# Values projected for four pairs of heads at once and kept in DRAM, and the rope's sine product taken before the halves are swapped

## The reference

```
hn = (h - mean) * rsqrt(var + 1e-5) * gamma + beta
q, k, v = hn @ Wq + bq, hn @ Wk + bk, hn @ Wv + bv        # 16 heads of 64
q, k = rope(q), rope(k)       # x * cos + concat(-x[32:], x[:32]) * sin, in each head
attn = softmax(causal(q @ k.T / 8))
x = layernorm(h + (attn @ v) @ Wo + bo + h)
gate, up = x @ (w_gate / 127).T, x @ (w_up / 127).T
x = layernorm(x + (silu(gate) * up) @ (w_down / 127).T + x)
```

## Time and profile before

| | |
|---|---|
| median of three runs | 2310.25 us (2309.42 to 2313.67) |
| profiled execution, its own time | 2305.9 us |
| its span in the profile | 2304.1 us |
| PE busy | 2144.3 us, 93% of the span |
| DVE busy | 1691.7 us, 73% |
| POOL busy | 1435.4 us, 62% |
| ACT busy | 958.2 us, 42% |
| granted TensorE clock, mean | 0.973 |

### The profile page before, as it was taken

One profiled execution on the slowest core, in us unless ns is written; L12 is line 12 of the kernel. 1 busy time (PEld: TensorE's weight loads), 2 busy tenths in 40 slices (PEclk: granted clock), 3 DMA queues, 4 the chain that ended last, 5 costly groups with the idle time before them and its releaser, 6 DMA issues.

```text
span 2304.1 us, 43543 instructions
## 1 busy us (share of the span) xinstructions
PE 2144.3 (93%) x15872; PEld 1407.3 (61%) x15872; DVE 1691.7 (73%) x2318; ACT 958.2 (42%) x1301; POOL 1435.4 (62%) x1204
## 2 busy tenths in 40 slices
PE   5779999999999999899999999999999999889997
PEld 4446565556565656455656565556565654789996
DVE  8567878787878787777877777787777775466654
ACT  3334444444434443434444444444344445333433
POOL 2447777777777777566868686878687779200000
PEclk8799999999999999989999999999999999899999
DMA  5100101010101011101111111111111130222200
GB/s 161 63 22 19 46 19 46 21 43 22 42 24 41 24 41 54 48 19 32 33 32 33 32 33 33 33 32 33 33 29 36 29 115 10 96 92 73 100 19 28
DMA packets 79484, 100.45 MB, mean 44 GB/s; under 512 B 13984, under 2 KB 43680, under 8 KB 79008
## 3 DMA queue, kind: packets, MB, share of 16 engines
q1 hardware_dynamic: 79264, 97.60, 14.2%
HBM read 40.93 MB, written 23.07 MB: 28 GB/s over the span
## 4 chain that ended last, share of the span: by engine, by line
PE 73%; DVE 17%; issue 6%; ACT 1%; DMA 1%; SPq 1%; POOL 1%; DVEq 0%; ACTq 0%
PE o_ps L1150 17%; PE m_ps L1098 8%; DVE mpart L748 6%; PE x_ps L1053 6%; PE s_ps L1119 4%; PE x_ps L1055 4%; PE x_ps L1054 4%; PE s_ps L1121 4%; PE s_ps L1125 4%; PE s_ps L1123 4%; PE gu_ps L1053 2%; PE gu_ps L1054 2%; PE gu_ps L1055 2%; PE x_ps L1157 1%; DVE rot L787 1%
## 5 line engine op out<-in xcount | busy, mean ns | idle before, releaser
L474 POOL TENSOR_TENSOR acc<-acc,pt 128x512 f32<-128x512 f32 (+3 forms) x1024 | 1235.4, 1238 | 232.6 <-ACT pt L533 232.0
L748 DVE TENSOR_REDUCE mpart<-m_ps 128x2 f32<-128x1024 f32 (+2 forms) x576 | 625.6, 1086 | 342.1 <-PE m_ps L1098 205.5
L533 ACT ACTIVATE pt<-s_ps 128x1024 f32<-128x1024 f32 (+3 forms) x640 | 545.1, 896 | 561.7 <-PE s_ps L1125 319.5
L1150 PE MATMUL o_ps<-pt,v 128*64 128x512 f32 (+3 forms) x2560 | 555.4, 556 | 0.0
L1098 PE MATMUL m_ps<-qk 64*128 64x512 f32 (+3 forms) x1280 | 285.8, 442 | 102.5 <-DVE mpart L748 85.1
L1098 PEld LDWEIGHTS m_ps<-qk 64*128 64x128 f32 x1280 | 121.8, 186 | 384.0 <-issue 217.3
L1150 PEld LDWEIGHTS o_ps<-pt,v 128*64 128x64 f32 x2560 | 158.5, 139 | 232.5 <-issue 211.4
L469 POOL TENSOR_TENSOR acc<-pt 128x512 f32<-128x512 f32 (+1 forms) x128 | 165.5, 1313 | 200.0 <-ACT pt L533 200.0
L1119 PE MATMUL s_ps<-qk 64*128 64x512 f32 (+3 forms) x1280 | 249.8, 385 | 0.0
L1121 PE MATMUL s_ps<-qk 64*128 64x512 f32 (+3 forms) x1280 | 235.9, 363 | 0.0
L1125 PE MATMUL s_ps<-aux,ones_r 64*128 64x512 f32 (+3 forms) x1280 | 235.8, 362 | 0.0
(11 more groups left out here) (161 smaller groups left out, 3406.7 us busy)
## 6 DMA issues: line engine op xcount, KB each, us to landing
rot<-qr SPq DMA_DIRECT2D x512, 64.0 KB, 2.0
attn<-o_n SPq DMA_DIRECT2D x64, 256.0 KB, 2.1
o_raw<-attn SPq DMA_DIRECT2D x8, 2048.0 KB, 9.0
w_raw<-in_wqkv SPq DMA_DIRECT2D x51, 128.0 KB, 2.6
h_g<-in_h SPq DMA_DIRECT2D x8, 512.0 KB, 3.6
out<-out_g SPq DMA_DIRECT2D x7, 512.0 KB, 2.9
qk_place<-in_h SPq DMA_DIRECT2D x4, 512.0 KB, 5.8
pt<-in_h SPq DMA_DIRECT2D x4, 512.0 KB, 10.6
```

The costliest lines, as they stand in the source:

```text
L474: nc.gpsimd.tensor_tensor(sums, sums, probs, ALU.add).then_inc(summed, 1)
L533: nc.scalar.activation(pt[:, u % SLOTS, :, q0:NB], s_ps[:, two:two + 2, q0:NB], ACT.Exp, scale=SCALE)\
L748: nc.vector.tensor_reduce(dst, m_ps[:, :, 0:w], AX.X, ALU.max, negate=True).then_inc(maxed, 1)
L1150: last = nc.tensor.matmul(o_ps[rows, q0:NB], v[par][:, j, rows], pt[:, u % SLOTS, a, q0:NB], start=(j == 0), stop=(j == n - 1), skip_group ...
```

## The change

It has four parts that go together.

1. **Values.** They are projected for four pairs of heads at once: one tile of 128 rows against 512 columns of `Wv` (six matmuls of 512 columns, `project_v`), 16 tiles for each set of four pairs, four sets in all. ACT brings a tile out of PSUM without its bias (`evict_v`) into one buffer, `v_part`, and SP stores it in DRAM, `v_far` (256 KB a tile). Each pair loads its own 128 columns of it, 12 tiles at group 1 of the pair before and 4 tiles at its own group 2 (`load_v`). The first set is projected ahead of pair 0, four tiles after each block; the second in pairs 0 to 3, one tile in each of the old places of values; the third, which needs the second batch row, in pair 7 alone (`SWITCH_PLACES`, 16 places); the fourth in pairs 8 to 11. Pairs 4 to 6 and 12 to 15 project no values. `Wv` has its own buffers and is split in two halves at a time (`WV_LOAD`, `WV_SPLIT`).
2. **Rope.** `products` on DVE takes both products straight out of PSUM, first the one with the sine into `qr` (its signs are now those of the half from which it comes), then the one with the cosine. The swap then carries a finished product, and in place of two instructions after the maxima there is one, the sum (`turned_sum`). ACT has no `piece_raw` any more.
3. **Bias of values.** The probabilities of a row sum to 1, so the bias is added to the result of attention, where it is split for the output projection (`attn_hi`, `attn_lo`).
4. **Unfolding.** `each_pair` has no hardware loops any more. The buffers `r_b` and `o_n` are gone: the division is made in place in `o_sum`, and ACT waits for the store of `o_sum` before it writes it again.

```diff
-VALUES = {g: int(x[1]) for g, x in XUSE.items() if x[0] == "V"}
+V_GROUPS = [g for g, x in XUSE.items() if x[0] == "V"]
+SWITCH_PLACES = [(3, 1), (4, 1), (5, 1), (7, 1), (8, 1), (9, 0), (9, 1), (10, 1), (11, 1), (13, 1), (14, 0), (14, 1),
+                 (15, 1), (16, 0), (16, 1), (17, 1)]
+V_PIECES = {it: {} for it in range(2 * PAIRS)}
+for it in range(4):
+    V_PIECES[it] = {(g, 0): (TT + 4 * it + i, 4 * it + i) for i, g in enumerate(V_GROUPS)}
+    V_PIECES[PAIRS + it] = {(g, 0): (3 * TT + 4 * it + i, 4 * it + i) for i, g in enumerate(V_GROUPS)}
+V_PIECES[PAIRS - 1] = {place: (2 * TT + i, i) for i, place in enumerate(SWITCH_PLACES)}
+WV_LOAD = {(0, 2): 2, (0, 5): 3, (5, 3): 4, (5, 6): 5, (8, 2): 6, (8, 5): 7}
+WV_SPLIT = {(0, 4): 2, (0, 7): 3, (5, 5): 4, (5, 8): 5, (8, 4): 6, (8, 7): 7}
...
-            pair(FIRST, 0, 0, 0, 0)
-            with engine.Fori(0, PAIRS // 2 - 1) as two:
-                pair(MIDDLE, two * 2 + 1, 1, two * 2 + 1, 0)
-                pair(MIDDLE, two * 2 + 2, 0, two * 2 + 2, 0)
...
+            kinds = {0: FIRST, PAIRS - 1: SWITCH, 2 * PAIRS - 1: LAST}
+            for it in range(2 * PAIRS):
+                pair(kinds.get(it, MIDDLE), it, it % 2, it % PAIRS, it // PAIRS)
...
+            def load_v(it, c0, c1, done):
+
+                here, cols = slice(TG * c0, TG * c1), slice(it % 4 * P, (it % 4 + 1) * P)
+                sp.dma_start(v[it % 2][:, here, :], v_far[it // 4, here, :, cols].rearrange("t p n -> p t n"))\
+                  .then_inc(done, 16)
+
+            def store_v(it, place):
+                if place in V_PIECES[it]:
+                    n, t = V_PIECES[it][place]
+                    sp.wait_ge(v_done, n + 1)
+                    sp.dma_start(v_far[n // TT, t, :, :], v_part[:, :]).then_inc(v_stored, 16)
...
                     if g in PIECE and kind is not LAST:
                         swap_halves(it + 1, *PIECE[g])
+                    store_v(it, (g, 0))
+                    store_v(it, (g, 1))
+                    if kind is SWITCH and g == 14:
+                        sp.wait_ge(v_stored, 16 * v_stored_for(it + 1, 2))
+                        load_v(it + 1, 0, 3, v_in)
...
-            def piece_raw(n, c, a, par, i, first=False):
...
-                act.wait_ge(qk_proj, n * (2 * BLOCKS) + (2 * c + a + 1))
-                nc.scalar.activation(qr[:, a, :], qk_bank[i][a], ACT.Identity, bias=b_qk[:, par, a:a + 1])\
-                  .then_inc(qk_raw, 1)
...
             def evict_o(n, blk):
                 act.wait_ge(pv_done, n * NG + (BLOCK_ENDS[blk] + 1))
-                act.wait_ge(normed, n * BLOCKS + (blk + 1))
+                act.wait_ge(o_stored, (n * BLOCKS + blk) * 16 + 16)
...
+            def evict_v(n, bank, dst):
+                act.wait_ge(v_proj, n + 1)
+                nc.scalar.activation(dst, bank, ACT.Copy).then_inc(v_done, 1)
...
+            def evict_v_piece(it, place):
+                if place in V_PIECES[it]:
+                    n = V_PIECES[it][place][0]
+                    if n > TT:
+                        act.wait_ge(v_stored, 16 * (n - TT))
+                    evict_v(n, x_ps[:, :], v_part[:, :])
...
-                nc.vector.tensor_tensor(v[par][:, TG * c:TG * (c + 1), :],
-                                        v_bank[i].rearrange("p (t n) -> p t n", t=TG),
-                                        b_v[:, par, :].unsqueeze(1).broadcast_to([P, TG, P]), ALU.add)\
-                  .then_inc(v_done, 1)
-
-            def cosine(n, c, a, par, i):
...
+            def products(n, c, a, par, i):
+
+                if c == 0 and a == 0:
+                    dve.wait_ge(b_in, n * 16 + 16)
+                dve.wait_ge(qk_proj, n * (2 * BLOCKS) + (2 * c + a + 1))
+                nc.vector.scalar_tensor_tensor(qr[:, a, :], qk_bank[i][a], b_qk[:, par, a:a + 1],
+                                               sin_sb[:, NB * c:NB * (c + 1)], ALU.add, ALU.mult).then_inc(qk_raw, 1)
...
-                nc.vector.tensor_tensor(rot[:, a, :], rot[:, a, :], sin_sb[:, NB * c:NB * (c + 1)], ALU.mult)\
-                  .then_inc(rope_mul, 1)
...
-            def project_v(n, c, i):
-                for t in range(TG):
-                    here = slice(NB * c + P * t, NB * c + P * (t + 1))
-                    for k in range(KC):
-                        last = product(v_bank[i][:, t * P:(t + 1) * P], [hn[:, x, k, here] for x in range(2)],
-                                       [w_hl[:, x, k, 2 * P:3 * P] for x in range(2)],
-                                       first=(k == 0), last=(k == KC - 1))
+            def project_v(n, t, bank):
+
+                pe.wait_ge(wv_lo, KC * (n // TT + 1))
+                here = slice(P * t, P * (t + 1))
+                for k in range(KC):
+                    last = product(bank, [hn[:, x, k, here] for x in range(2)], [wv_hl[:, x, k, :] for x in range(2)],
+                                   first=(k == 0), last=(k == KC - 1))
```

More of the change, by code:

```diff
@@ L225, in postln_block_kernel @@
         v_done = sem("v_done")
+        v_put = [sem(f"v_put{i}") for i in range(4)]
+        v_stored = sem("v_stored")
+        v_in = sem("v_in")
+        v_in3 = sem("v_in3")
+        wv_in = sem("wv_in")
+        wv_hi = sem("wv_hi")
+        wv_lo = sem("wv_lo")
         m_scored = sem("m_scored")
@@ L599, in next_hi @@
                   .then_inc(a_hi, 1)
-            def raw(c):
-                for a in range(2):
-                    piece_raw(0, c, a, 0, c % 2, first=(c == 0))
             def rounded(c):
@@ L613, in _ @@
             act.wait_ge(ln_in, 16 * 3)
-            for i in range(4):
-                affine(i)
+            affine(0)
+            affine(1)
+            split_wv(0, wv_raw[:, :])
+            split_wv(1, v_part[:, :])
+            affine(2)
+            affine(3)
             root_input(3)
-            raw(0)
+            evict_v_first(0)
             affine(4)
             affine(5)
-            raw(1)
+            evict_v_first(1)
             affine(6)
@@ L837, in pair @@
                     if g - 1 in PIECE and kind is not LAST:
-                        cosine(it + 1, *PIECE[g - 1], 1 - par, 2)
-                    if g - 1 in VALUES and kind is not LAST:
-                        values(it + 1, VALUES[g - 1], 1 - par, 2)
+                        products(it + 1, *PIECE[g - 1], 1 - par, 2)
                     for m in group_maxima(kind, g):
@@ L877, in unturned @@
                 for a in range(2):
-                    cosine(0, c, a, 0, c % 2)
-                values(0, c, 0, c % 2)
+                    products(0, c, a, 0, c % 2)
             def turned(c):
                 for a in range(2):
-                    sine(0, c, a)
+                    turned_sum(0, c, a)
             def remainders(c):
@@ L896, in _ @@
             rest(1)
+            rest_wv(0, wv_raw[:, :])
+            rest_wv(1, v_part[:, :])
             input_group(3)
@@ L1161, in pair, with shared_free @@
                 nxt = kind is not LAST
-                def shared_free(g):
-                    for before in range(g - 1, -2, -1):
-                        x = XUSE[before % NG]
-                        n, i = (it if before >= 0 else it - 1), int(x[1])
-                        if x[0] in "QKV" and nxt:
-                            if x[0] == "V":
-                                pe.wait_ge(v_done, n * BLOCKS + (BLOCKS + i + 1))
-                            else:
-                                pe.wait_ge(cos_done, n * (2 * BLOCKS) + (2 * BLOCKS + 2 * i + "QK".index(x[0]) + 1))
+                def shared_free(g, behind):
+                    for place in range(2 * (NG * it + g) + behind - 1, -1, -1):
+                        n, b, late = place // (2 * NG), place // 2 % NG, place % 2
+                        if (b, late) in V_PIECES[n]:
+                            pe.wait_ge(v_done, V_PIECES[n][b, late][0] + 1)
@@ L1173, in shared_free @@
                             return
[L1174 to L1176 removed]
+                        if late and b in SUMMED and (n, b) != (0, 0):
+                            pe.wait_ge(r_turned, (n - 1 if b == 0 else n) * BLOCKS + (SUMMED[b] + 1))
                             return
[L1178 to L1180 removed]
+                        if not late and b in PIECE and n < FINAL:
+                            c, a = PIECE[b]
+                            pe.wait_ge(cos_done, (n + 1) * (2 * BLOCKS) + (2 * c + a + 1))
@@ L1181, in shared_free, with values_piece @@
                             return
+                        if not late and b in TURN_M and (b < NG - 1 or n < FINAL):
+                            pe.wait_ge(aux_done, (n + (b == NG - 1)) * BLOCKS + (TURN_M[b] + 1))
+                            return
+                    pe.wait_ge(aux_done, 1)
+                def values_piece(g, behind):
+                    if (g, behind) in V_PIECES[it]:
+                        n, t = V_PIECES[it][g, behind]
+                        if it >= PAIRS - 1:
```

(3 more changed lines are left out.)

197 lines of the change are left out of this document (111 added, 86 removed).

## The result

| | before | after |
|---|---|---|
| median of four runs each | 2310.91 us | 2258.71 us (2253.5 to 2262.26) |
| profiled execution, its own time; its span | 2305.9; 2304.1 | 2253.5; 2251.6 |
| granted clock, mean | 0.973 | 0.968 |

The ratio is 0.9771, with a 95% interval of 0.9747 to 0.9795: the kernel is 52 us faster. 2281 had been forecast, -29.5; the range held the time, and the forecast's own part of it (2262 to 2300) did not.

The account below looks back on a forecast made before the run. PE was taken as the bound, waiting at times for DVE's maxima. Middle pairs -17.5 and -30, loops -9, pair 7 +12, opening +4, splits +2, clock +9 make -29.5: 2310.25 to 2281 us; range 2236 to 2310.

Parts of the forecast that it names:

- 1. Values on PE: Projecting values with 512-column matmuls takes PE 102 us instead of 180, saving 79.
- 2. How much of it reaches the end: Middle pairs: net -2.5 us in each of seven with tiles, -5 in each of six without values.
- Groups 4 and 5: First maximum of this stretch at 484.8 instead of 484.15, PE waiting 2.1 us, not 1.43: 0.65 us lost per pair.
- Groups 8 to 13: PE 1.25 us late at group 9 and some 1.3 us late at group 13, in both kinds of pair.
- Groups 14 to 19: Forecast as groups 14 to 18: PE regains 3.7 us with tiles; without values 8.5, less 2.2 for DVE.
- shorter sums: Sign against the forecast: DVE's sums, 1.64 us in its working and 1.36 on average before, get shorter.
- The first rival: All of PE's saving counts, -79 and -9: 2222 us, up to 2240 with pair 7's waits; chance 0.17.
- 3. Other work on DVE, ACT and SP: Bias, copies, stores and loads cost nothing; the six splits of `Wv` cost +2 us, bounds 0 and 4.
- 4. Pair 7: Pair 7, with 14.2 us more PE work and waits on `v_part` and SP: +12 us, bounds 0 and 25.
- 5. Opening and pair 0: PE has 14.2 us more ahead of pair 0, largely set by DVE and transfers: +4, bounds -3 and 16.
- 6. Loops: Unfolding saves 2.2 us at each of four loop turns: -9 us, bounds -5 and -9.
- 7. Clock: Middle pairs: five more stretches at clock 0.50, 1.7 us each: +9 us, bounds 0 and 26.

Follow-up runs that it names:

- e6: Kernel after, with the third set's value tiles moved: 12 in pair 7, none directly behind a rope piece in its group, 4 in pair 8; 2244.91 us.
- e1: Kernel before with its 16 pairs written out one by one instead of hardware loops, nothing else; 2303.5 us, ratio 0.997.

## Why the prediction was right or wrong, by its steps

**1. Values on PE: right.** PE's busy time fell by 67 us, without what the clock cost by 77 (2082 to 2005), forecast 79, and a pair without values now holds 100.7 us of it where 111.5 were: 10.8, forecast 11.3. The formula that I weighed against this, of the Trainium skill ("TensorE: Matmul & The Clock Gate", Back-to-back issue gap), would have left PE 3 us in all; the trace doesn't agree. The section gives that formula for a matmul by itself. For a stream of loads and matmuls it gives 81 and 131 ns; by these the saving is 74 us (an estimate), near what came, though the starts here are 117 and 265 ns apart.

**2. How much of it reaches the end: the step that failed, in its size.** Net -17.5 and -30 had been forecast for the 13 middle pairs, with loops and clock -47.5; they gave -74.1. At the clock of 1.00 a pair with tiles gained 4.3 where 2.5 stood, and one without 7.7 where 5 stood. The lengths of the groups, in us, in three pairs at 1.00:

| groups | before, pair 3 | tiles, pair 2 | no values, pair 14 | forecast |
|---|---|---|---|---|
| 4, 5 | 11.66 | 11.86 | 11.87 | +0.65 |
| 8 to 13 | 34.72 | 34.24 | 34.02 | PE +1.3 late at 13 |
| 14 to 19 | 38.16 | 34.43 | 31.20 | -3.7 and -6.3 |
| the others | 30.05 | 29.66 | 29.63 | 0 |

- *Groups 4 and 5* went as followed step by step. In pair 14 of after:

```profile
1727.42 0.74 DVE L855 SCALAR_TENSOR_TENSOR qr<-x_ps,b_qk,sin_sb 128x512 f32<-128x512 f32 x1
1732.01 1.51 DVE L866 TENSOR_TENSOR qc<-qc,rot 128x512 f32<-128x512 f32 x1 [0.95 <-DMA rot<-qr]
1736.92 0.50 PE L1175 MATMUL m_ps<-qk 64*128 64x512 f32 x2 [1.54 <-DVE mpart L828]
```

  The sum starts 4.59 us behind the product, forecast 4.6. PE waits 1.54, not 2.1: from the first product to PE's next start it is 9.5 us here and 9.3 in the earlier trace rows, so 0.2 was lost and not 0.65.
- *Groups 8 to 13* carried the error. I had PE 1.25 us late at group 9, and the block's saving there used up by DVE. Group 8 is 0.15 us longer (6.15 for 6.00). Group 9 gives the saving in full, 5.97 us with a tile and 4.39 without where 7.22 stood, and groups 10 and 11 take 0.6 and 2.0 of it back. That a tile or nothing in group 9 makes little difference was right; but PE comes to group 13 0.3 and 0.5 us early (counted from group 4) and not 1.3 late. That is 1.6 and 1.8 us in each pair of the two kinds. (Whether the 0.65 is in the 1.3 the working leaves open; the net figures hold 1.3 alone.)
- *Groups 14 to 19* came near: 3.7 with tiles as forecast, 7.0 without where 6.3 stood. But the reason for the 2.2 that I took off doesn't hold. I took "6.3 us long on DVE", 0.74 + 3.9 + 1.64, for the bound of every group with a sum. These 6.3 us are a latency, not work: the products are made under `weigh` of one group, DVE then reduces two maxima while the swap travels, and the sum falls under `weigh` of the next. In pair 14 groups 14 to 18 are 4.35, 5.99, 4.45, 5.87 and 4.56 us long, and PE doesn't wait in any of them. It waits in group 10 and in group 19 (5.97 us for 4.45):

```profile
1764.48 0.51 PE L1175 MATMUL m_ps<-qk 64*128 64x512 f32 x2 [1.84 <-DVE mpart L828]
1812.30 0.38 PE L1175 MATMUL m_ps<-qk 64*128 64x256 f32 x2 [1.75 <-DVE mpart L828]
```

- *The sum* was sized at 1.64, from one row beside POOL; it is 1.13 in the mean, from 1.02 in the rows of group 16 to 1.51 in those above. I had named shorter sums as what would prove me wrong.

The first rival, that all of PE's saving counts, was nearer for pairs with tiles (5.1 for the 4.3 that came) and further off for those without (11.3 for 7.7).

**3. Other work on DVE, ACT and SP: right in kind**, not measured apart. No wait of ACT for a store of `v_part` is in the trace.

**4. Pair 7: mis-sized, +22 where +12 stood,** inside its bounds, and for another reason. I blamed `v_part` and SP's queue; ACT waits for PE there, not for the store. The busy time of PE rose by 16.6 us (14.2 the work, the rest the clock, 0.91 for 0.94) and its idle time by 5.4: 12.5 us of waits behind rope pieces in `x_ps` are new, and the waits for `mpart` fell from 13.7 to 6.6. e6, in which no tile stands behind a piece, shows that cause: pair 7 at 133.2.

**5. Opening and pair 0:** -1.7 where +4 stood, within the bounds.

**6. Loops:** -7 (interval -11 to -2) in e1, forecast -9, and -5 can't be told from it. In its trace pairs 2 and 4 fell from 118.3 and 118.4 to 116.0 and 116.8, while pairs 1 and 3 rose from 114.7 and 114.5 to 116.0, with clock 0.99 for 1.00: part of the gain went there.

**7. Clock:** the mean of 0.973 and 0.968 over the spans is 62 and 72 us lost, +10, forecast +9. The 13 middle pairs lose 8.5 more (12 to 20.5), as forecast. Pair 7 loses 5 more, which I hadn't counted, and what stands ahead of pair 0 loses 5 less. (There are 13 middle pairs, not the 14 of that step.)

The errors of steps 2 (-27) and 4 (+10) partly cancelled. That the forecast came within 1% of the result owes something to that.

## What to carry to other kernels

Where two engines hand one buffer back and forth, add up for each gap between two handovers what stands in it on either side; only the longer side counts, and a cut on one of them is worth what the other then leaves. Two cuts that are each worth little or less than nothing can be worth a lot together, so neither is judged alone. Before a run is read as "this work removed", look up in its profile how much of the engine's time went with it. And split what a run gains or loses into PE's work, its idle time and the clock: here the clock was a third to a half of what a dead instruction cost. A latency that spans several gaps isn't a bound on any of them; and before a job is moved to fill a wait, look at what already stands in the gap where it lands, and at who must read the bank that it writes.
